# Keeping the blocks and the products of a block inversion in PSUM banks

## The reference

```
def _step(S, xs):
    qt, kt, vt, gt, bt = xs
    S = S * jnp.exp(gt)[..., None, None]
    pred = jnp.einsum('bhk,bhkv->bhv', kt, S)
    delta = (vt - pred) * bt[..., None]
    S = S + jnp.einsum('bhk,bhv->bhkv', kt, delta)
    return (S, jnp.einsum('bhk,bhkv->bhv', qt, S))
...
x = x + attention(xn) + feed_forward(xn)
```

## Time and profile before

| | |
|---|---|
| median of three runs | 1183.21 us |
| lowest and highest run | 1177.44, 1183.7 us |
| span of the profiled execution | 1191.3 us |
| TensorE busy | 969.3 us (81%) |
| VectorE busy | 712.9 us (60%) |
| ScalarE busy | 456.7 us (38%) |
| GpSimd busy | 344.3 us (29%) |

### The profile page before, as it was taken

The page is one execution under the profiler, slowest core; times in us unless marked ns, Lnnn a source line. Parts: engine busy times, 40 slices in busy tenths (PEclk is TensorE's granted clock), DMA queues, the critical chain, the costliest instruction groups (busy, mean ns, idle before and its releaser), DMA issues. The chain is left out here.

```text
span 1191.3 us, 16665 instructions
## 1 busy us (share of the span) xinstructions
PE 969.3 (81%) x5592; PEld 578.1 (49%) x5592; DVE 712.9 (60%) x1455; ACT 456.7 (38%) x1038; POOL 344.3 (29%) x351
## 2 busy tenths in 40 slices
PE   4897298989298989657989829974677999999988
PEld 2453286564187645257746428741132444444433
DVE  5799656667745676944676864442986328064250
ACT  3635224436223444512443622422574226053140
POOL 1558201465400255700136630006804000000000
PEclk9889599979797989968898969886678999999999
DMA  7221300101220201040100030006055111100101
GB/s 222 80 66 35 89 1 23 59 1 28 48 70 3 80 1 27 1 115 4 46 36 11 18 71 10 19 27 192 18 185 151 54 53 36 45 26 18 53 11 43
DMA packets 70560, 61.77 MB, mean 52 GB/s; under 512 B 48059, under 2 KB 52028, under 8 KB 70470
## 3 DMA queue, kind: packets, MB, share of 16 engines
q1 hardware_dynamic: 62526, 41.42, 12.3%
q0 software_dynamic: 4224, 13.37, 3.6%
q10 hardware_dynamic: 3720, 5.85, 1.4%
HBM read 38.08 MB, written 23.13 MB: 51 GB/s over the span
## 5 line engine op out<-in xcount | busy, mean ns | idle before, releaser
L2035 DVE SCALAR_TENSOR_TENSOR yr<-pd,yr 128x512 f32<-128x512 f32 x16 | 11.1, 692 | 146.4 <-PE pd L1831 146.4
L1829 PE MATMUL pd<-dw,it 128*128 128x512 f16 x256 | 97.0, 379 | 1.5 <-DVE it L2030 1.5
L1919 ACT ACTIVATE sg<-pg 128x512 f32<-128x512 f32 x64 | 37.7, 591 | 157.1 <-PE pg L1820 145.2
L659 PE MATMUL bank<-Tbd,BA 128*128 128x128 f32 x192 | 32.1, 332 | 80.9 <-DMA Tbd<-t_blocks 80.9
L1830 PE MATMUL pd<-dw,it 128*128 128x512 f16 x256 | 97.0, 379 | 0.0
L1831 PE MATMUL pd<-dw,it 128*128 128x512 f16 x256 | 97.0, 379 | 0.0
L982 DVE TENSOR_TENSOR tmp<-bin,tin 96x60 f32<-96x60 f32 (+32 forms) x184 | 87.3, 500 | 15.4 <-DMA bin<-b_blocks 13.1
L988 DVE TENSOR_TENSOR tin<-tin,tmp 96x60 f32<-96x60 f32 (+32 forms) x184 | 82.1, 471 | 3.1 <-DVE tmp L982 0.7
L1729 POOL DMA_DIRECT2D yr<-y_attn x16 | 8.7, 546 | 251.3 <-DMA out<-yr 251.3
L557 PE MATMUL bank<-x_hi,w_hi 128*128 128x512 f16 x192 | 76.1, 397 | 3.0 <-DVE x_lo L864 1.5
L557 PE MATMUL bank<-x_lo,w_hi 128*128 128x512 f16 x192 | 75.3, 392 | 0.0
(11 more groups left out here) (249 smaller groups left out, 2473.9 us busy)
## 6 DMA issues: line engine op xcount, KB each, us to landing
xb<-in_x SPq DMA_DIRECT2D x4, 1024.0 KB, 5.7
xr<-in_x SPq DMA_DIRECT2D x16, 256.0 KB, 2.7
y_attn<-xr SPq DMA_DIRECT2D x16, 256.0 KB, 2.0
down_rows<-dn SPq DMA_DIRECT2D x4, 1024.0 KB, 8.0
yr<-y_attn POOLq DMA_DIRECT2D x16, 256.0 KB, 2.9
out<-yr SPq DMA_DIRECT2D x16, 256.0 KB, 2.0
xn_hi<-x_hi POOLq DMA_DIRECT2D x4, 512.0 KB, 4.5
xn_lo<-x_lo POOLq DMA_DIRECT2D x4, 512.0 KB, 5.5
```

The lines of the kernel that those rows point to most:

```text
L659: ins = nc.tensor.matmul(ps[:, 128 * h:128 * h + 128], BA[:, 0, i, :], Tbd[:, i, :], start=True, stop=True)
L1829: nc.tensor.matmul(ps[:], it_hi[:, i, tok], dw[:, i, 0, :], start=i == 0, stop=False)
```

## The change

`tmp` leaves SBUF. After the wait for `b_in`, two new copies bring the two halves of the 96 x 1024 block data from `bin` into banks 4 and 5, 96 x 512 each. The products go to bank 6. So the product reads its column of the block from a bank and the row of the inverse from SBUF and writes a bank, and the subtraction reads `tin` from SBUF and the product from a bank and writes `tin` in SBUF. The first product waits for the second copy instead of the second memset. The semaphore's count in a stage grows by two. The transposing copy at the end still writes `bin`.

```diff
-        tmp = sb("tmp", [NINST, 5 * SUB * SUB // 16])
...
+        INV_BANKS = (4, 5, 6)
...
                 dve.wait_ge(t32_step, step(v.memset(tin[:], 0.0)))
-                ones = step(v.memset(tin[:, 0:SUB * SUB:SUB + 1], 1.0))
+                step(v.memset(tin[:, 0:SUB * SUB:SUB + 1], 1.0))
                 dve.wait_ge(b_in, s.val(16, 16))
+                rows_in = SUB * SUB // 2
+                for k in range(2):
+                    copied = step(v.tensor_copy(bank[INV_BANKS[k]][0:NINST, :], bin_[:, rows_in * k:rows_in * (k + 1)]))
                 tv = tin[:].rearrange("p (i c) -> p i c", i=SUB)
                 half = SUB // 2
-                done_to = [ones, ones]
+                done_to = [copied, copied]
+                tmp = bank[INV_BANKS[2]]
...
-                            prod = tmp[:, half * half * k:half * half * k + n * (c1 - c0)]
+                            prod = tmp[0:NINST, half * half * k:half * half * k + n * (c1 - c0)]
...
+                    row = bank[INV_BANKS[2 * j // SUB]][0:NINST, SUB * (j % half) + j + 1:SUB * (j % half) + SUB]
                     for k, c0, c1, prod in todo:
                         dve.wait_ge(t32_step, done_to[k])
                         done_to[k] = step(v.tensor_tensor(
-                            prod, bin_[:, SUB * j + j + 1:SUB * j + SUB].unsqueeze(2).broadcast_to([NINST, n, c1 - c0]),
+                            prod, row.unsqueeze(2).broadcast_to([NINST, n, c1 - c0]),
                             tv[:, j, c0:c1].unsqueeze(1).broadcast_to([NINST, n, c1 - c0]), ALU.mult))
...
-T32_STEPS = 3 + 2 * (SUB - 1) + SUB - 2
+T32_STEPS = 5 + 2 * (SUB - 1) + SUB - 2
```

## The result

| | before | after |
|---|---|---|
| median, both measured again on one chip | 1180.33 us (1175.55 to 1183.7) | 1112.13 us (1110.78 to 1115.54) |
| span of the profiled execution | 1191.3 us | 1110.3 us |
| TensorE, VectorE busy | 969.3, 712.9 us | 964.9, 644.0 us |
| ScalarE, GpSimd busy | 456.7, 344.3 us | 455.9, 335.3 us |

The ratio is 0.9418, interval 0.9383 to 0.9453: 68.7 us less (64.6 to 72.8). The prediction said 1108 us, 75.2 us less than the before of that time. The time lies within the forecast's own range (1097 to 1115); the gain is 6.5 us smaller, and 75.2 lies outside its interval.

The account below looks back on a forecast made before the run. The prediction took VectorE's block inversion, held by GpSimd, as the bound in every stage. Stage gains of 15.5, 18.8, 19.0 and 18.9 us (72.2) plus 3 for the clock gave 75.2 us less: 1108 us, own range 1097 to 1115, 8-in-10 range 1096 to 1134.

Parts of the forecast that it names:

- What bounds: In every stage the block inversion on VectorE is the path; TensorE idles 17.73 to 21.31 us before the solve.
- The holds go, all of them: GpSimd's holds on VectorE's inversion steps all vanish: 20 us a stage, 17 in stage 0.
- Undisturbed length: The inversion steps on VectorE without holds take 22.1 us a stage: 12.0 plus 9.8 plus 0.3 for gaps.
- Reading PSUM: In the inversion steps on VectorE, an input from a PSUM bank instead of SBUF costs nothing extra.
- Writing PSUM: The 46 products a stage writing a bank cost nothing extra, bounded by 0.125 us each, 5.8 us a stage.
- The rival with a fixed price: PSUM costs 0.06 us on each of 92 inversion steps, 22 us over four stages: 1130 us; chance 0.13.
- Copies 1.33 us: Two added 512-element copies from SBUF to PSUM before the inversion steps lengthen the path by 1.33 us a stage.
- The transfer way: From the end of the inversion steps to the first solve matmul: 7.9 to 8.3 us, by stage.
- The last copy: The copy after the inversion (L991) may be held by one GpSimd instruction, 1.3 us, at no cost to the path.
- What is late next: TensorE's own work ends 2.0 to 2.3 us before the new solve starts; a cheaper inversion gains at most 8.7 us.
- The clock: With less idle time TensorE may stay at 2.4 GHz in the solve: 5.7 us in all, half taken, 3.
- The predicted span: Whole profiled execution: 1191.3 us becomes 1116.1 us; the median was taken to stay 8.1 us below the span.

Follow-up runs that it names:

- the kernel with the shorter inversion: The changed kernel with columns 16 to 30 of the inversion left out, so the inverse is incomplete: 1079.11 us, ratio 0.9242 to the kernel before.
- the small copies: The changed kernel with the two large copies replaced by row-by-row copies behind the first chain's products: 1094.99 us, ratio 0.9362 to before; again 1094.41 us, 0.9354.

## Why the prediction was right, point by point

- **What bounds.** Right. TensorE waits for Tbd in all stages, before and after, so the 71.9 us taken from the inversions are taken from the path.
- **The holds go, all of them.** Right, shown from both sides: one input in a bank removes them (no step over 0.43 us), and so does the absence of GpSimd's additions. The row that carried it was rows 8, another line in the same situation. The prediction put all 19 holds of a stage down to the additions; one of them is the masking of the weights. In the changed kernel it comes behind the steps (in stage 1 at 290.95 us), so no trace shows it beside a step with an input in a bank.
- **Undisturbed length, 22.1 us.** Measured 22.2, and 21.9 in stage 0.
- **Reading PSUM, nothing.** Right: the subtractions take 272 ns on average, against 275 for the same ones unheld in SBUF (the kernel without the additions).
- **Writing PSUM, nothing, bounded by 0.125 us.** Right within a third of a microsecond: the products, which read and write a bank, take 281 ns against 274, 0.3 us a stage on 46. ScalarE's difference of rows 10 is no guide to VectorE. The rival with a fixed price would have needed 0.06 us on every step. The Trainium skill, "VectorE: DVE Perf Modes", section on the TRN2 errata, gives a higher fixed cost for an instruction that reads PSUM than for one that reads SBUF; neither this row nor the comparison of 22.2 with 22.4 us shows it.
- **Copies 1.33 us.** Measured 1.31 to 1.32, never held. Part of that was luck: L1086, called a one-source price, has two inputs, a bank and `xr`.
- **The transfer way, 7.9 to 8.3 us.** Measured 7.90 to 8.37.
- **The last copy, perhaps held once, harmless.** It took 2.00, 1.07, 1.60 and 2.10 us where it took 1.03: held in three stages, though it has one SBUF input. Where VectorE comes first, GpSimd's instruction is held instead: the addition at 283.60 took 2.14 us beside the copy at 283.53. The copies into banks, one SBUF input too, are not held. The Trainium skill, "SBUF — State Buffer", section "Who interferes with whom", excepts the modes that use both ports from its rule for one SBUF input (the prediction left the exception out): in them VectorE contends with GpSimd, and whoever comes first blocks the other. By the Trainium skill, "VectorE: DVE Perf Modes", section "Mode 2×_2P — use both read ports for one tensor", that mode is for tensors in SBUF alone. The traces agree with both. The copy was harmless, but not because only the second store needs it: SyncE issues the loads of Tbd behind that store, so they wait for the copy too. In the changed kernel the copy ended 0.9 us or more before the first store had landed. In stage 0 of the kernel with the shorter inversion it took 3.36 us and the loads were issued only at 112.26 us, 0.83 behind that landing.
- **What is late next: TensorE's own work, 2.0 to 2.3 us earlier.** 2.35 to 3.82 in the first trace, 3.00 to 9.66 in the two later ones. The prediction took the end of TensorE's work from one trace as fixed. In stages 1 to 3 it lies 27.3 to 30.2 us behind the start of the inversion in two traces of the kernel before, and 26.5 to 28.9 in three of the changed one; in stage 0 it is 29.1 in the first trace and 21.6 and 22.5 in the later ones. GpSimd's additions beside the steps take 1.27 us instead of 1.32 to 1.35; how much of the earlier end is due to that isn't shown. The half inversion gained 11.5 us in all where 8.7 was the cap.
- **The clock, 3 of 5.7 us.** The mechanism is there, and irregular. The first twelve matmuls took 2.93, 1.92, 1.60 and 2.09 us instead of 2.92 or 2.93 four times, 3.2 us less in all. In the two later traces they took 2.93, 1.60, 2.92, 2.93 and 2.93, 2.92, 2.93, 1.89 us, only 1.3 and 1.0 less. Windows before and behind the start of the solve, stage 0 and stage 2 of the changed kernel (columns as in rows 4):

```profile
108.00:114.00 6.00, 1.39 (x7) 0.42 (x5) 5.98 (x31) 2.93 (x6) 5.84 (x7) 0.81 0.00 1
114.00:118.00 4.00, 3.94 (x13) 1.96 (x14) 3.90 (x31) 0.48 (x2) 3.84 (x6) 0.50 0.00 0
118.00:122.00 4.00, 0.83 (x5) 0.53 (x3) 1.95 (x1) 3.00 (x5) 1.04 (x1) 0.93 0.64 179
122.00:126.10 4.10, 1.13 (x5) 0.73 (x5) 0.00 (x0) 2.83 (x10) 3.75 (x4) 0.50 1.15 172
126.10:132.30 6.20, 6.20 (x28) 6.03 (x28) 1.67 (x3) 2.08 (x7) 1.77 (x1) 0.50 0.81 196
...
450.00:458.00 8.00, 7.26 (x39) 3.58 (x37) 4.65 (x25) 5.57 (x10) 7.65 (x8) 1.00 0.40 110
458.00:461.10 3.10, 0.60 (x5) 0.36 (x4) 0.69 (x1) 2.40 (x9) 3.02 (x3) 1.00 1.19 171
...
461.20:464.50 3.30, 3.30 (x29) 3.18 (x29) 1.67 (x3) 1.43 (x5) 1.93 (x2) 1.00 1.00 206
```

In stage 0 TensorE was busy for only 1.39 of the 6 us before 114, and the clock fell to 1.2 GHz. From 118 to 122 it was back at 2.4 for the most part. Then it was at 1.2 again, TensorE being busy for 1.13 of 4.1 us, and the solve begins at 1.2 GHz: 28 matmuls in 6.20 us. In stage 2 TensorE had been busy for 7.26 of 8 us, then for 0.60 of 3.1, and stayed at 2.4 GHz: 29 matmuls in 3.30 us, with an idle time of about the same length ahead. From the first solve matmul to the first of L669 it is 22.05 us before and 19.44 after, in all stages together; in the later traces of the changed kernel 20.4 and 22.0, in the second one of the kernel before 19.6, with the small copies 17.9. So the idle time that the change shortens is only one of the things that the clock hangs on. The 3 us came in one trace of three, and the scatter between traces is as large.

**The step that failed** is the last one, from terms to microseconds. The 8.1 us between profiled span and median were carried over as fixed; the changed kernel's span lies 1.8 us below its median, then 7.3 above and 1.5 below it when measured again, that of the kernel before, run again, 3.6 below. The predicted span, 1116.1 us, was 5.8 us too long, and the distance from there to the median was 9.9 us off the other way; that the time fell within the range all the same is in part luck. What moves the span is the part outside the inversions. In five profiles, span less inversions:

| | span | inversions | the rest |
|---|---|---|---|
| before | 1191.3 | 198.3 | 993.0 |
| before, again | 1162.0 | 196.7 | 965.3 |
| after | 1110.3 | 126.4 | 983.9 |
| after, again | 1105.3 | 126.0 | 979.3 |
| after, third | 1098.7 | 125.8 | 972.9 |

The rest scatters over 28 us without order between the kernels, above all behind the last solve. The gain by ratio is 68.7, 69.3 and 68.8 us in three measurements, the inversions give 71.9, 70.7 and 70.9 in the traces. The term-wise sum without a clock term, 72.2 us, lies in the first interval (64.6 to 72.8), the predicted 75.2 outside. Whether the 1 to 3 us between the inversions and the ratios are lost somewhere, or are scatter, stays open: no view here separates them from the rest's own movement.

## To carry over

Where VectorE and GpSimd both read SBUF at the same time, look in the timeline for single instructions that are far longer than their neighbours of the same size, and end shortly behind an instruction of the other engine; their number follows the other engine's instructions, so half a cure gives less than half, and all the steps of a chain must be freed. In this kernel one input in PSUM freed a VectorE product or subtraction that has two, in either place, and cost nothing measurable but the way there; small independent copies fitted into the waits of the dependent chain for free. Make the sum from the stretches that the change touches, and compare ratios of medians: the distance from a profiled span to the median is no constant.

## What was not expected of the hardware

- 23 small copies a stage (164 to 194 ns each) inside a chain of dependent steps cost at most 0.04 us. The chain leaves time free, since a step of 31 elements has 0.19 us and its successor can't start earlier, while an independent instruction starts 0.10 us after it.
- Freeing only the products brought 16.1 us, freeing only the subtractions 15.1, both 70.7.
- Two copies of 0.7 us put on the path cost 1.34 and 1.36 us in two stages, and the whole kernel nothing measurable (0.9996), since the steps of the other two stages met fewer of GpSimd's additions, in stage 0 mostly for another reason than the copies.
- VectorE's copy of 1024 elements within SBUF, 1.03 us alone, was held up to 2.10 us by GpSimd and held GpSimd by 0.87 us (2.14 instead of 1.27), the only instruction of the changed inversion that does either. GpSimd's additions lost only 0.05 to 0.08 us each to the small steps that they held for a microsecond.
